# Second attention layer: the norm's factor on POOL, and the product that uses it on DVE, moved to the second quarter of the following period

## The reference, cut to what matters

```python
x = x + _L1_attn_ref(_layernorm(x), Wq, Wk, Wv, Wout)     # causal softmax(q k^T / sqrt(8)) v, then Wout
x = x + _L1_ffn_ref(_layernorm(x), norm_w, w1, w3, w2, gate_w, a1, b1, a3, b3, a2, b2)

def _layernorm(x, eps=1e-5):
    return (x - mean(x)) / sqrt(var(x) + eps)
# _L1_ffn_ref begins with an RMS norm of what it is given:
nx = x * rsqrt(mean(x * x) + 1e-6) * norm_w
```

## Time and profile before

| | before |
|---|---|
| median of 3 runs | 996.12 us (994.94 to 998.17) |
| the profiled execution's own time | 995.86 us |
| its span, first to last instruction | 993.9 us |
| mean granted TensorE clock | 0.966 |
| busy: PE | 880.1 us (89%) |
| busy: DVE | 758.9 us (76%) |
| busy: ACT | 523.0 us (53%) |
| busy: POOL | 456.0 us (46%) |
| periods 0 to 7 of `attention1` | 425 to 708 us of the span |

### The profile page before, as it was taken

The page is one execution under the profiler, slowest core; times in us unless marked ns, Lnnn a source line. Parts: engine busy times, 40 slices in busy tenths (PEclk is TensorE's granted clock), DMA queues, the critical chain, the costliest instruction groups (busy, mean ns, idle before and its releaser), DMA issues. The chain is left out here.

```text
span 993.9 us, 18285 instructions
## 1 busy us (share of the span) xinstructions
PE 880.1 (89%) x6457; PEld 580.8 (58%) x6457; DVE 758.9 (76%) x1499; ACT 523.0 (53%) x772; POOL 456.0 (46%) x601
## 2 busy tenths in 40 slices
PE   5799999997777784689999999997889999999997
PEld 4677777783665553444444454453547667766775
DVE  5888889966899993888888989987676666656642
ACT  4577777896345454257776677766622223122220
POOL 4122222224566666226555655535553454355344
PEclk9899999998999998779999999999989999999999
DMA  9100000000000005554434434300000000000000
GB/s 293 51 12 12 11 11 11 11 1 0 5 1 12 1 12 118 133 125 105 108 77 110 109 69 106 74 3 14 12 0 22 1 22 21 21 0 21 11 11 11
DMA packets 35637, 43.33 MB, mean 44 GB/s; under 512 B 4825, under 2 KB 27769, under 8 KB 35569
## 3 DMA queue, kind: packets, MB, share of 16 engines
q1 hardware_dynamic: 35569, 42.43, 17.4%
HBM read 21.21 MB, written 15.07 MB: 37 GB/s over the span
## 5 line engine op out<-in xcount | busy, mean ns | idle before, releaser
L1707 ACT ACTIVATE PT<-PS 128x1024 f32<-128x1024 f32 x160 | 162.7, 1023 | 71.0 <-PE PS L1491 70.7
L1761 POOL TENSOR_SCALAR_AFFINE_SELECT PT<-PT 128x256 f32<-128x256 f32 (+1 forms) x224 | 97.2, 450 | 128.0 <-ACT PT L1707 126.5
L2175 POOL TENSOR_TENSOR PRE_sb<-PRE_sb,VA 128x512 f32<-128x512 f32 x64 | 82.6, 1292 | 139.8 <-DVE PRE_sb L2241 139.7
L2138 ACT ACTIVATE sg_d<-PS 128x512 f32<-128x512 f32 x64 | 38.3, 598 | 176.6 <-PE PS L1231 176.6
L2241 DVE TENSOR_TENSOR PRE_sb<-sg_d,PS 128x512 f32<-128x512 f32 x64 | 43.4, 687 | 79.8 <-ACT sg_d L2138 78.5
L1506 PE MATMUL PS<-PT,VA 128*32 128x512 f32 (+3 forms) x1024 | 91.2, 453 | 11.6 <-POOL PT L1761 11.6
L426 ACT ACTIVATE E<-PS,m 128x512 f32<-128x512 f32 x128 | 85.7, 689 | 27.8 <-PE PS L314 19.1
L1798 DVE TENSOR_REDUCE negm<-PS 128x2 f32<-128x1024 f32 x64 | 77.9, 1222 | 17.9 <-PE PS L1480 16.9
L1476 PE MATMUL PS<-kS,qS 48*128 48x384 bf16 (+3 forms) x512 | 74.9, 316 | 17.9 <-DVE spread L1934 9.7
L471 POOL TENSOR_SCALAR Qs<-Qs 128x1024 f32<-128x1024 f32 x32 | 34.3, 1071 | 107.0 <-ACT Qs L407 107.0
L1801 DVE TENSOR_REDUCE negm<-PS 128x2 f32<-128x768 f32 x64 | 61.2, 956 | 9.3 <-PE PS L1480 7.8
(11 more groups left out here) (312 smaller groups left out, 2274.0 us busy)
## 6 DMA issues: line engine op xcount, KB each, us to landing
qk_rows<-parts SPq DMA_DIRECT2D x32, 192.0 KB, 2.8
qS<-qk_rows SPq DMA_DIRECT2D x32, 192.0 KB, 4.1
kS<-qk_rows SPq DMA_DIRECT2D x32, 192.0 KB, 4.5
xs_sb<-XN_sb SPq DMA_DIRECT2D x23, 256.0 KB, 2.3
qk_rows<-parts SPq DMA_DIRECT2D x32, 128.0 KB, 2.8
X_sb<-in_x_dram SPq DMA_DIRECT2D x8, 256.0 KB, 6.4
qk_rows<-parts SPq DMA_DIRECT2D x32, 64.0 KB, 2.5
out_dram<-X_sb SPq DMA_DIRECT2D x8, 256.0 KB, 2.3
```

Source lines behind the costliest of these rows:

```text
L1707: nc.scalar.activation(PT[:, quad % 2, u, :], PS[:, b:b + 2, :].rearrange("p b n -> p (b n)"), ACT.Exp).then_inc(exp_ready, 1)
L1761: nc.gpsimd.affine_select(out=v, in_=v, pattern=[[0, 4 if u == 4 else 2], [1, P]], compare_op=ALU.is_ge, fill=0.0, base=0, channel_multipl ...
L2175: nc.gpsimd.tensor_tensor(acts[:, s, f, :], acts[:, s, f, :], W[:, slot, s, :], ALU.mult).then_inc(weighted, 1)
```

## The change

On POOL, `factor(i - 1)` at step (3, 1) of periods 1 to 6 becomes `factor(i - 2)` at step (1, 0) of periods 2 to 7: the same six factors, half a period later. On DVE, `apply(i - 2)` moves within the same periods from step (1, 1) to step (1, 4). No instruction is added, removed or altered.

```diff
@@ gpsimd, period(i, slot)
-                    if (quad, u) == (3, 1) and not (first or last):
-                        factor(i - 1)
+                    if (quad, u) == (1, 0) and i > 1:
+                        factor(i - 2)
                     elif (quad, u) == (0, 1) and behind(i):
                         pr.third_part(pool, i + 2, 1)

@@ vector, period(i, slot)
                     elif (quad, u) == (3, 1) and not first:
                         aggregate(i - 1)
-                    elif (quad, u) == (1, 1) and i > 1:
+                    elif (quad, u) == (1, 4) and i > 1:
                         apply(i - 2)
```

## The result

| | before | after |
|---|---|---|
| median | 996.65 us (4 runs) | 984.18 us (4 runs, 982.77 to 986.64) |
| the profiled execution | 995.86 us | 982.77 us |
| its span | 993.9 us | 980.8 us |

The ratio is 0.9878 with a 95% interval of 0.9848 to 0.9908; in a second set of five runs it was 0.9874 (0.9855 to 0.9892). By the medians the kernel became 12.5 us faster; the forecast was 12.8.

A forecast was written before the change was run, and what follows sets the result against it. PE was taken as bound by POOL's late selects at period starts, by its own work in between. Terms 9.8 + 3.8 + 0.3 - 0.7 - 0.4 = 12.8 us gave 983.3 us from the median, range 981.0 to 989.0.

The forecast's parts named there:

- Period starts of 2 to 6: Windows over these starts fall to period 1's 7.39 us once the factor leaves (3, 1): 9.8 us gained.
- Start of period 7: PE's 2.74 us wait for POOL's select and 1.1 us of slow running behind it vanish: 3.8 us gained.
- Factor at (1, 0): POOL's chain at its new step costs nothing, 1.3 us to spare in period 3; up to 0.3 us in period 7.
- Apply at (1, 4): DVE's new step: free in periods 2 to 4 and 6; 0.7 us lost in period 5, 0.4 in period 7.
- Apply away from (1, 1): Second quarters of periods 2 to 5 shorten by 0.07 us each: 0.3 us gained.
- A, the clock: Clock dips at the starts of periods 3 and 7, 2.1 us, come back elsewhere: 985.4 us; chance 0.15.
- B: DVE becomes the bound: moved apply costs PE up to 1.11 us in each of periods 2 to 6; 988.2 us, chance 0.15.
- C: Backlog only moves to the second quarter; gain eaten at 7.1 us chain length, 1001.7 us at 8; chance 0.03.
- D: Nothing happens, because another engine ends the wait at the period starts: 996 us; chance 0.05.

The follow-up runs named there:

- run that kept the wait: Kernel before with the factor's chain at (3, 1) replaced by one short product, POOL's wait for DVE's statistics kept, factor values wrong; ratio 0.9865, span 981.2 us.
- apply-only run: Kernel before with only the apply moved from (1, 1) to (1, 4), the factor left at (3, 1); ratio 1.0007, span 994.2 us.
- factor-only run: Kernel before with only the factor moved from (3, 1) to (1, 0), the apply left at (1, 1); ratio 1.0021, median 998.16 us.

## Why the prediction was right, point by point

The mechanism was right in each term. That the sum agrees to the tenth is partly luck: period 7's start was 0.25 us and period 5 0.14 us better than forecast, the second quarters 0.06 and the moved apply in period 7 0.34 us worse, and these cancel. The sum also counts two clock dips, 2.1 us, as gained, which nothing in the profile of before could promise; the changed kernel's second profile has one dip in the stage again.

*Period starts of 2 to 6.* Forecast 9.8 us, measured 9.81: all five take the 7.39 us of period 1. The control inside the profile of before, one period that lacks what is to be removed, carried the whole term. That the chain and not the wait made the backlog is shown by the run that kept the wait.

*Start of period 7.* Forecast 3.8, measured 10.43 - 6.38 = 4.05 us, within the bound of 4.1. The apply-only run splits it by accident: 9.19 us with the wait but without the dip, so 2.8 us of wait and 1.2 of clock, near the 2.7 and 1.1 of the forecast. This rests on one profile of each kind.

*Factor at (1, 0).* Forecast as free, with 1.3 us to spare in period 3; measured 1.36, with a chain of 3.63 us and no wait of PE for POOL. The runs with one and three more `pow` show the cover from both sides.

*Apply at (1, 4).* Nothing in periods 2 to 4, as forecast. Period 5: forecast 0.7, measured 0.56. Period 7: forecast 0.4, measured 7.13 - 6.39 = 0.74, all of it in PE's wait for the copy (0.93 us against 0.2 before). Here the term was mis-sized: the step took the 1.11 to 1.29 us of an apply with little beside it (the prediction says that the apply of the earlier trace rows ran without any select; it ran beside 0.15 us of one), and four instructions took 1.73 us, since the factor's chain had pushed POOL's selects into the same 2.5 us. The upper bound of 1.9 us lost had named this case. The changed kernel's second profile is close to a control: the same four instructions, with 0.78 us of selects beside them instead of 1.65, took 1.19 us, and the quarter 6.60 us, so the apply cost 0.21 there. In periods 2 to 7 of all profiles the apply takes 1.10 to 1.11 us with none to 0.15 us of selects beside it, 1.19 to 1.30 with 0.35 to 0.8, 1.30 to 1.49 with 1.0 to 1.5, and 1.54 to 1.73 with more; beside 1.03 us of POOL's `pow` alone (period 7 of the run with three more) it takes 1.10. The Trainium skill (SBUF — State Buffer, Who interferes with whom) has such pairs wait for one another; the trace agrees in direction only, since 1.11 us of apply and 1.65 us of selects, each waiting out the other, would need 2.8 us, and took 1.73. That a shared port is the reason is argued, not shown.

*Apply away from (1, 1).* Forecast 0.3 us, measured 0.06 in each of four quarters, 0.2.

*The rivals.* A, the clock: the profiled execution had no dip in the stage window, the second profile had one of 1.5 us, so the forecast's bound of 2 us was of the right kind; the changed kernel's runs scatter from 982 to 987 us. The prediction speaks of four like waits at the period starts; there were five (1.60, 1.37, 1.37, 1.37 and 1.49 us), one of them followed by a dip. B did not occur at (2, 0), but the factor-only run shows DVE as a bound elsewhere: delayed by 2.5 us at (1, 1) it costs PE 1.8. C was wrong in its break-even of 7.1 us: at a chain of 6.8 us the stage window is already 9.7 us longer than before (254.21 against 244.56). It priced the stalls at 6 x (6.8 - 3.64 - 1.3) = 11 us where they took 13.7, since period 7 has almost no cover, and it left out the 8.8 us of slow clock behind them. D is refuted by the windows over all six period starts.

## What to carry to other kernels

An engine that is busy 46% of the time can still be the one that others wait for, if its work comes in one place; look for the period that lacks the suspect and use it as the control. Moving a producer into a quiet stretch is half a change: its consumer has to be late enough to find it done, and early enough that what queues behind the consumer is not late. A stall of the matrix engine may cost more than its own length, so the cover over a moved piece is worth measuring: one more `pow` here was nearly free in five of six periods (0.8 us in all), three more cost 22 us.

## What was not expected of the hardware

The price of a stall depends on what TensorE's clock does next. Before, PE stalled five times for 1.4 to 1.6 us at like places, and the granted clock fell below its full level of 2.4 GHz, for a part at 1.2, after one of them, worth 1.0 us. At the start of period 7 a stall of 2.74 us was followed by a dip in the profile of before and by none in that of the apply-only run. In the factor-only run it fell after two of four stalls of about 1.85 us, 1.4 us each, and not after a fifth of 1.4; with the longer chain after five of six, 1.0 to 2.9 us each, and the one without a dip (2.10 us) was longer than the 1.64 us of period 6 with the dearest dip. In the undisturbed stage window it stayed at 2.4 GHz for 231 us. The same kernel's second profile has one dip there, just behind a wait of 1.21 us that both profiles have. So the length of the last stall alone does not decide it; what does stays open.
